# Scores of the first attention group's maxima are computed twice into the same place on TensorE

## The reference, cut to what matters

```python
q, k, v = split(layernorm(x) @ w_attn.T)          # 32 heads of 16, rope on q and k
scores = einsum('bhqd,bhkd->bhqk', q, k) / sqrt(16)
scores = where(causal, scores, -inf)
attn = softmax(scores, axis=-1)                   # exp(scores - max) / sum
y = einsum('bhqk,bhkd->bhqd', attn, v)            # + the gated adapter attention
x = x + layernorm(y @ w_proj.T)
x = x + layernorm(silu(xn @ W_gate.T) * (xn @ W_up.T) @ W_down.T)
```

## Time and profile before

| what | value |
|---|---|
| time of the kernel, median of 3 runs | 1222.85 us |
| lowest and highest of them | 1222.13 and 1223.36 us |
| time of the profiled execution | 1222.75 us |
| span in its trace, first to last instruction | 1221.0 us |
| PE busy | 1113.5 us, 91% of the span |
| DVE busy | 713.0 us, 58% |
| mean granted TensorE clock | 0.938 of 2.4 GHz |

### The profile page before, as it was taken

How to read it: one execution, slowest core, us unless ns; L and a number is a source line. 1 busy time by engine, 2 the same in 40 slices (tenths; PEclk the granted TensorE clock), 3 DMA queues, 4 the chain that set the end, 5 groups by cost and what they waited for, 6 DMA issues and landing times. The chain is left out here.

```text
span 1221.0 us, 18084 instructions
## 1 busy us (share of the span) xinstructions
PE 1113.5 (91%) x7020; PEld 758.8 (62%) x7020; DVE 713.0 (58%) x983; ACT 493.4 (40%) x1042; POOL 252.4 (21%) x251
## 2 busy tenths in 40 slices
PE   3999999898999999999799989389999999999996
PEld 1877778544555455545455434277787887887884
DVE  4756646767788877887677536277534324324113
ACT  3233232335777777777577635112421111111110
POOL 3625438201311111111011124143001001001001
PEclk9999999758999999999799778788999999999998
DMA  6356777553444444444444115544411101100100
GB/s 243 104 141 174 165 178 180 115 105 58 88 88 88 80 80 80 81 81 80 84 81 127 56 58 168 143 129 134 149 50 45 59 1 40 65 1 33 37 1 35
DMA packets 93869, 113.08 MB, mean 93 GB/s; under 512 B 26456, under 2 KB 54744, under 8 KB 93784
## 3 DMA queue, kind: packets, MB, share of 16 engines
q1 hardware_dynamic: 91928, 108.21, 34.9%
q10 hardware_dynamic: 1856, 3.71, 1.9%
HBM read 68.82 MB, written 42.21 MB: 91 GB/s over the span
## 5 line engine op out<-in xcount | busy, mean ns | idle before, releaser
L835 ACT ACTIVATE prob<-ps_s 128x512 f32<-128x512 f32 (+3 forms) x768 | 323.7, 496 | 194.6 <-PE ps_s L982 187.9
L857 DVE TENSOR_REDUCE neg<-ps_m 128x2 f32<-128x1024 f32 (+2 forms) x224 | 248.3, 1145 | 61.1 <-PE ps_m L947 38.6
L982 PE MATMUL ps_s<-q_op,k_op 50*128 50x512 f32 (+2 forms) x768 | 246.3, 457 | 18.6 <-ACT prob L835 14.0
L947 PE MATMUL ps_m<-k_op,q_op 48*128 48x512 f32 (+2 forms) x768 | 187.1, 423 | 15.5 <-DVE neg L857 12.6
L982 PEld LDWEIGHTS ps_s<-q_op,k_op 50*128 50x128 f32 x768 | 120.0, 196 | 123.3 <-ACT prob L835 59.9
L794 POOL TENSOR_SCALAR_AFFINE_SELECT prob<-prob 128x512 f32<-128x512 f32 x128 | 82.1, 642 | 433.8 <-ACT prob L835 433.7
L996 PE MATMUL ps_y<-prob,vg 128*17 128x512 f32 (+3 forms) x1536 | 158.7, 536 | 0.0
L1536 DVE TENSOR_TENSOR hf<-sl,ps_u 128x512 f32<-128x512 f32 (+1 forms) x44 | 30.2, 686 | 170.6 <-PE ps_u L78 153.4
L947 PEld LDWEIGHTS ps_m<-k_op,q_op 48*128 48x128 f32 x768 | 98.3, 201 | 34.0 <-DVE neg L857 25.6
L857 DVE TENSOR_REDUCE neg_far<-ps_m 128x4 f32<-128x512 f32 (+2 forms) x96 | 100.3, 1048 | 30.9 <-PE ps_m L952 29.3
L1601 PE MATMUL ps_d<-w_high,wp_high 128*128 128x512 f32 (+1 forms) x352 | 115.2, 390 | 1.1 <-DVE wp_high L1538 1.1
(11 more groups left out here) (168 smaller groups left out, 1702.8 us busy)
## 6 DMA issues: line engine op xcount, KB each, us to landing
y_heads<-y_sb SPq DMA_DIRECT2D x32, 256.0 KB, 2.0
raw<-in_w_ffn SPq DMA_DIRECT2D x31, 256.0 KB, 3.5
k_op<-k_parts SPq DMA_DIRECT2D x28, 256.0 KB, 4.5
q_op<-q_parts SPq DMA_DIRECT2D x56, 128.0 KB, 5.1
v_groups<-v_out SPq DMA_DIRECT2D x16, 272.0 KB, 4.4
x<-in_x SPq DMA_DIRECT2D x4, 1024.0 KB, 8.0
q_parts<-part_h SPq DMA_DIRECT2D x16, 256.0 KB, 2.9
q_parts<-part_l SPq DMA_DIRECT2D x16, 256.0 KB, 2.9
```

Source lines behind the costliest of these rows:

```text
L835: act.activation(prob[:, v % NPROB, h, unit_cols(u)], ps_s[:, y % NS, unit_cols(u)], ACT.Exp, scale=D ** -0.5).then_inc(s_exp, 1)
L857: nc.vector.tensor_reduce(to[:, :, pairs[0]:pairs[-1] + 1, i - TT * c], scores, axis=AX.X, op=ALU.max, negate=True).then_inc(a_read, 1)
L947: last = nc.tensor.matmul(ps_m[:, g % 2, s, base:base + wide], q_op[buf][r, c, pair, (i - TT * c) * P:(i - TT * c + 1) * P], k_op[buf][r, ...
L982: nc.tensor.matmul(ps_s[:, y % NS, lo:BLK], k_op[buf][r, pair, j * P:(j + 1) * P], q_op[buf][r, c, pair, lo:BLK], start=True, stop=True)\
```

## The change

Before the matmuls of a piece, `max_scores` now first issues matmuls of the same operands, with the same width, into the same place of `ps_m`. Each begins a new sum (start=True), as the real one behind it does, so the real one overwrites what the repeated one wrote. `repeated(g)` tells how many: two (s = 0 and s = 1) for 6 <= g < 19; one (s = 0) for the other g from 11 up to `at[(2, LEAD)]` = 56; none before and behind. Only the first pair of heads of a piece is repeated. A turn doesn't go through `max_scores`, and gets nothing.

```diff
+        def repeated(g):
+
+            if 2 * len(early) <= g < first_main + 8:
+                return range(2)
+            return range(1 if first_main <= g < at[(2, LEAD)] else 0)
+
         def max_scores(g):
...
             free_slot(g)
+            for s in repeated(g):
+                r = slice(64 * s, 64 * s + KQ)
+                nc.tensor.matmul(ps_m[:, g % 2, s, 0:wide], q_op[buf][r, c, pairs[0], (i - TT * c) * P:(i - TT * c + 1) * P],
+                                 k_op[buf][r, pairs[0], lo:lo + wide], start=True, stop=True)
             for x, pair in enumerate(pairs):
```

## The result

The changed kernel is slower. Its median is 1230.59 us (13 runs, 1223.96 to 1233.67) against 1222.13 us of the kernel before beside it (13 runs, 1216.84 to 1226.74). The ratio is 1.0059, interval 1.0037 to 1.0082. The forecast was 1216.5 us, and its range ended at 1227.0.

The account below looks back on a forecast made before the run. It took DVE to set the pace in the changed stretch as long as PE keeps up, though PE is busiest on average. An early clock rise shortening DVE's waits gave +0.4 and savings, together -6.3 us: 1216.5 us, range 1211.5 to 1227.

Parts of the forecast that it names:

- The clock falls near 226 in spite of the repeats: First group's start: repeats fill 0.21 us in each of three waits, the 1.95 us DMA wait stays, the clock still falls.
- So I place it nearer to the first, by little: Doubled pieces g = 11 to 14, about 228 to 234: dense like the products, so the clock rises by about 233.
- rival 3: First group: clock stays where it was, PE at 1.2 GHz becomes the bound; +4.7 us, 1227.5 us; chance 0.22.
- a run without a break raises the clock: Nearest row for the doubled stretch: the run of 16 products, after which the clock rose at 253.6.
- At the full clock the 8.3 us of repeats cost nothing: g = 7 to 55 at 2.4 GHz: all added PE work, 8.3 us, is covered by DVE's reductions.
- unmasked pieces just covered, masked ones 1.7 us late by 244: At 1.2 GHz: unmasked piece 1.07 us of PE; masked g = 15 to 23 add 2.7 us against 0.96 idle.
- The sum: Forecast, first group: clock low from 226 to about 233, high to 284; DVE's waits shrink, together -6.3 us.
- its second term: DVE's waits for PE between 234 and 250, counted as eight, halve: -1.5 of 3.0 us.
- That gains or losses carry to the end unchanged: Behind 295 us nothing is added and later work starts from the shifted work, so the gain carries to the end.
- The first term: Up to 244, at 1.2 GHz: added work exceeds PE's idle time, +1.7 us.
- The second: 257.1 to 274.1: some ten pieces get about 3.3 us of steps against 1.1 us idle, +2.2 us.
- The third: 284.4 to 294.6: six pieces get 2.6 us against 0.9 idle, half of the rest beside DVE, +0.8 us.

Follow-up runs that it names:

- e4: Kernel after without any repeats, but with 8 pairs of dummy matmuls in the DMA wait ahead of the first scores; 1.0021 of the kernel before.
- e3: Kernel after with all its repeats, plus 8 pairs of dummy matmuls in the DMA wait ahead of the first scores; 1.0048 of the kernel before.
- e1: Kernel after with only the two repeats of g = 7 to 18, the single ones left out; 1.0015 of the kernel before.
- e2: Kernel after with only the single repeats of g = 19 to 55, the double ones left out; 1.0054 of the kernel before.
- e7: Kernel after with four repeats on unmasked and two on masked pieces, g = 7 to 55, and seven dummy pairs in the DMA wait; 0.9979 of before.
- e10: As e7, but four repeats also on masked pieces k = 2 and 3 around the turns and two on g = 7; 0.9966 of the kernel before.
- e11: Kernel after with only the 33 single repeats, moved to g = 129 to 165 (about 380 to 430 us); 1.0060 of the kernel before.
- e15: Kernel after with only the two repeats on the unmasked pieces g = 7 to 14; 1.0037 of the kernel before, 7 runs.
- e8: Kernel after with only the single repeats on the 20 masked pieces of g = 19 to 55; 1.0048 of the kernel before.
- e14: The same kernel as e8, unchanged, run and traced a second time; 1.0036 of the kernel before.
- e12: The kernel after, unchanged, compared with the kernel before a second time; 1.0055 of the kernel before.

## Why the prediction was wrong, point by point

**The clock falls near 226 in spite of the repeats: right.** It fell at 230.3, 5.7 us behind the first turn (before: 4.1), at the end of the same wait. PE's timeline, kernel after, answers to the earlier trace rows:

```profile
227.75 0.50 PE L949 MATMUL ps_m<-k_op,q_op 48*128 48x512 f32 x2 [0.40 <-DVE neg L857]
...
230.20 0.74 PE L992 MATMUL ps_s<-q_op,k_op 50*128 50x512 f32 x2 [1.72 <-DMA q_op<-row]
230.68 0.69 PE L949 MATMUL ps_m<-k_op,q_op 48*128 48x512 f32 x2
231.11 0.69 PE L957 MATMUL ps_m<-k_op,q_op 48*128 48x512 f32 x2
231.53 0.69 PE L949 MATMUL ps_m<-k_op,q_op 48*128 48x512 f32 x2
231.96 0.69 PE L957 MATMUL ps_m<-k_op,q_op 48*128 48x512 f32 x2
232.39 0.69 PE L992 MATMUL ps_s<-q_op,k_op 50*128 50x512 f32 x2
233.12 0.80 PE L949 MATMUL ps_m<-k_op,q_op 48*128 48x512 f32 x2
233.71 0.63 PE L957 MATMUL ps_m<-k_op,q_op 48*128 48x512 f32 x2
234.25 0.79 PE L949 MATMUL ps_m<-k_op,q_op 48*128 48x512 f32 x2
234.84 0.63 PE L957 MATMUL ps_m<-k_op,q_op 48*128 48x512 f32 x2
```

The 0.64 us for DVE became 0.40, as costed (one step of 0.21), and the DMA wait stayed. That this wait alone is the reason is not borne out: filled without repeats (e4) it didn't hold the clock, filled together with them (e3) it did.

**"So I place it nearer to the first, by little": this step failed, and with it the forecast.** I took the doubled stretch of g = 11 to 14 for work almost without a break, like the run of products, and let the clock rise by 233. It stayed at 0.50 to 284.9. The assumption was checkable by the starts of the matmuls rather than by busy time. Two adjacent pairs that do not wait start some 0.43 us apart, as in the rows from 230.68 to 232.39. That run, six pairs with the scores at both ends, is as dense as I had assumed for the whole stretch, and the clock didn't rise behind it. But it is over after 2.6 us. From 233.12 on, the starts are 0.59 and 0.54 us apart, 1.13 us for a piece that has two steps of 0.425 us: the piece still goes at DVE's pace, and 0.28 us in each are not work. Yet the timeline prints no idle time, and the stretch reads 10.14 busy of 10.20, because the profile gives a pair 0.80 or 0.63 us of busy time where the step is 0.425, and these times overlap. I had the 1.13 us at hand and used it only to cost the cover. e4 fits: there eight pairs stood one behind the other, 3.57 us in all, under 0.45 us each, and the clock rose. e1, where only these pieces are doubled, gave the same three low stretches as the kernel before. That this thinness is the cause is my reading; that the doubled pieces don't bring the clock back is shown.

The rise behind the first product went missing as well, in both traces of after, which no case of the prediction had: rival 3 left the low stretches where they were. The row that answers to the earlier trace rows and the first product of the earlier trace rows is

```profile
256.17 3.19 PE L1006 MATMUL ps_y<-prob,vg 128*17 128x512 f32 x16
```

The stretch around it has PE busy 5.60 of 5.60 us at 0.50, and the clock didn't rise until 284.9. In e1 and in e2 it rose behind the same product, and in e4, which has no repeats, it didn't. So my nearest row for "a run without a break raises the clock" isn't a rule either, and the missing rise can't be put down to the repeats as such. What decides here is not settled.

**At the full clock the 8.3 us of repeats cost nothing: right for this stage** (e7 and e10 carry more than twice as many and are shorter), wrong for a later one (e11).

**At the low clock, unmasked pieces just covered, masked ones 1.7 us late by 244: about right, by e15** (+0.2 us for the unmasked) and by the waits of after. From 237.30 to 254.45 there are ten waits for PE, which together make 4.6 us. The prediction counted eight waits and 3.0 us for the same work before; the timeline has seven, of 2.6 us in all. So they grew by 2.0.

**The sum.** Its terms were worked for a clock that never came. (With seven waits of 2.6 us in place of eight of 3.0, its second term is -1.3 instead of -1.5, which changes nothing.) The wait at the product, to fall from 3.06 to 1.46, rose to 3.67, and 3.42 rose to 4.57. -6.3 us became +7.8 in the stage.

**Rival 3 is what happened,** to the mechanism: the clock stayed low, PE became the bound, 13.90 of 13.90 us busy in 271 to 284.9. Its size was too small. Its three terms against the two traces, from the earlier trace rows and the rows of DVE above:

| part | rival 3 | measured |
|---|---|---|
| first turn to the first product's wait (222.22 to 254.55; 224.60 to 260.55) | +1.7 | 35.95 - 32.33 = +3.6 |
| from there to the row that waited 3.42 (to 275.61; 285.30) | +2.2 | 24.75 - 21.06 = +3.7 |
| from there to 297.09 and 306.09 | +0.8 | 20.79 - 21.48 = -0.7 |
| behind it, to 360.60 and 371.20 | 0 | 65.11 - 63.51 = +1.6 |

The first term counted only up to g = 23. The pieces from there up to the product, and the product's wait itself (+0.6), were left at their old cost. The second took as given the full clock of 274.1 to 284.4, which the earlier trace rows shows and which the added work pushed back. The third is a small gain; the clock was at 1.00 from 284.9 to 295.1. The fourth goes with low stretches that the kernel before doesn't have there, 295.1 to 302.0 and another of 3.4 us from 329.3 on, where nothing is added. All terms but the third miss to the same side. My reading is that I let the additions change PE's load and not the clock that goes with it: after is at 0.50 for 10.3 us longer, and that much made 3.5 us between e8 and e14. The range ended at 1227, with half of the rival left outside.

**That gains or losses carry to the end unchanged: right.** The rest is 858 us in both traces of after, within the 855 to 860 of before.

**The page's rule** of the Trainium skill ("TensorE: Matmul & The Clock Gate", section "Why this matters for your kernels"), that keeping TensorE busy regains the full clock, would have had it back in 230.3 to 240.5, with PE busy 10.14 of 10.20 us by the profile. The trace disagrees, as it did in the earlier trace rows, if busy is read from the profile's busy time; I gave the row of 233.2 to 243.8 too little weight.

## What to carry to other kernels

Filler work on TensorE paid here only where the granted clock really changed; short of that it is plain load on the engine that has just become the bound, and costs what that engine's idle time doesn't cover. Judge whether PE works without a break by the distance between the starts of its matmuls, and not by busy time, and size the filler for the whole stage with its turns and DMA waits: 57 matmuls in part of it (this change) lost 0.6%, 152 over all of it (e10) won 0.3%. Where one stage has changed, measure it between two instructions that exist in every variant, and in more than one trace of each: here such a stage repeats to between 0.2 and 3.5 us where the totals scatter by 10.

## What the runs showed of the hardware

**The time goes with the mean clock, in the same kernel.** Over the executions of one program the time falls by some 10 us for each 0.01 of mean granted clock: 10.2 us with a correlation of -0.93 in 26 executions of the kernel before (1216.6 to 1228.4 us), 11.5 and -0.94 in 35 others (1213.8 to 1227.9 us). Most of the spread in each set goes with it. In e12's comparison the kernel after has 0.938 on average where before has 0.940, which by this slope is 2 us of its loss of 5.7; the other 4 or so come at equal mean clock. e10 has 0.958, and wins 4.9 us where the slope alone would give 20: by this slope, the filler costs back most of what the clock gives.

**The clock moves outside the changed stage too.** In the 18 traces the rest behind the stage takes 854 to 862 us, and is at 0.50 for 77 us (e4, rest 854) to 97 us (before, rest 860) of it; the two go together with a correlation of 0.86, though no instruction there differs but in e11. This is where much of the scatter of the totals comes from.

**Work that looks nearly unbroken by busy time can stay at 1.2 GHz for 54.6 us,** with PE busy 10.14 of 10.20 us in one part of it and 13.90 of 13.90 in another, and one and the same run of products was followed by a rise in the earlier trace rows, e1 and e2, but not in after, e12 and e4.

**The same kernel can have another pattern of the clock.** e8 and e14 are one program, with 54.6 and 64.9 us at 0.50 and 3.5 us between their stages.
